# Two drained releases per group instead of seven attached ones, and a second buffer for the histogram operands

## The reference, cut to what matters

```python
h = batch_norm(x @ w1.T + b1, g1, bt1)
src, dst = (edge_index[0], edge_index[1])      # dst is sorted
diff = h[src] - h[dst]
m = jax.ops.segment_max(diff, dst, num_segments=N)
```

## Time and profile before

| | us |
|---|---|
| median of 3 runs | 3649.25 (3648.39 to 3667.12) |
| span of the profiled execution, first to last instruction | 3634.8 |

### The profile page before, as it was taken

The page is one execution under the profiler, slowest core; times in us unless marked ns, Lnnn a source line. Parts: engine busy times, 40 slices in busy tenths (PEclk is TensorE's granted clock), DMA queues, the critical chain, the costliest instruction groups (busy, mean ns, idle before and its releaser), DMA issues. The chain is left out here.

```text
span 3634.8 us, 41575 instructions
## 1 busy us (share of the span) xinstructions
PE 2966.5 (82%) x15504; PEld 2461.7 (68%) x15504; DVE 2207.0 (61%) x4089; ACT 1962.2 (54%) x2741; POOL 1496.1 (41%) x1530
## 2 busy tenths in 40 slices
PE   6578777787877778788887777728988999999998
PEld 5456565665665656566665666527878999999998
DVE  6576666666666666666666666540885556555544
ACT  5356555555555655555555555415165565566554
POOL 1566565565666655556665555561410000000000
PEclk9789898898898998889898898868999999999999
DMA  7355555555555555455555555450213324333331
GB/s 227 114 195 196 181 197 187 194 197 182 194 191 189 189 169 170 167 169 181 170 183 169 171 176 171 160 204 25 61 75 98 118 105 135 128 115 115 115 109 69
DMA packets 164927, 559.97 MB, mean 154 GB/s; under 512 B 31190, under 2 KB 68374, under 8 KB 157556
## 3 DMA queue, kind: packets, MB, share of 16 engines
q1 hardware_dynamic: 87492, 355.23, 26.1%
q0 software_dynamic: 77232, 202.08, 19.5%
HBM read 320.19 MB, written 237.00 MB: 153 GB/s over the span
## 5 line engine op out<-in xcount | busy, mean ns | idle before, releaser
L648 POOL DMA_INDIRECT ring<-runs,src_i x1436 | 1410.4, 982 | 1004.2 <-DVE ring L815 518.7
L999 PE MATMUL ps<-oh,zhl 128*128 128x512 f32 x3136 | 1347.5, 430 | 321.9 <-issue 159.7
L1001 PE MATMUL ps<-oh,zhl 128*128 128x512 f32 x3136 | 1308.0, 417 | 12.8 <-issue 12.5
L670 ACT ACTIVATE oh<-ids,nodeneg 128x512 fp32r<-128x512 f32 x896 | 633.6, 717 | 900.7 <-PE ps L1001 487.4
L999 PEld LDWEIGHTS ps<-oh,zhl 128*128 128x128 f32 x3136 | 642.1, 205 | 515.2 <-issue 186.4
L815 DVE SCALAR_TENSOR_TENSOR ring<-ring,pen 128x256 f32<-128x256 f32 x1564 | 750.4, 480 | 63.5 <-DMA ring<-runs,src_i 32.3
L821 DVE TENSOR_SCALAR oh<-ps,nodef 128x512 fp32r<-128x512 f32 x672 | 501.7, 747 | 403.6 <-PE ps L1001 248.5
L1001 PEld LDWEIGHTS ps<-oh,zhl 128*128 128x128 f32 x3136 | 643.2, 205 | 146.1 <-issue 15.3
L675 ACT ACTIVATE oh<-oh,ones 128x512 fp32r<-128x512 f32 x896 | 613.6, 709 | 0.0
L827 DVE TENSOR_TENSOR oh_lo<-lo,ps 128x896 bf16<-128x896 bf16 x224 | 242.8, 1084 | 328.7 <-remote 302.3
L1569 ACT ACTIVATE av<-ps,vecs 128x896 f32<-128x896 f32 x224 | 246.3, 1100 | 330.4 <-PE ps L191 330.4
(11 more groups left out here) (294 smaller groups left out, 3872.2 us busy)
## 6 DMA issues: line engine op xcount, KB each, us to landing
runs<-ring SPq DMA_DIRECT2D x136, 896.0 KB
fw<-wsp SPq DMA_DIRECT2D x56, 1536.0 KB, 6.5
runs<-ring SPq DMA_DIRECT2D x102, 768.0 KB
ring<-runs,src_i POOLq DMA_INDIRECT x1436
ids<-srcT_d SPq DMA_DIRECT2D x32, 256.0 KB
res_d<-x_all SPq DMA_DIRECT2D x7, 896.0 KB
y<-res_d SPq DMA_DIRECT2D x7, 896.0 KB, 7.0
part<-in_Wx SPq DMA_DIRECT2D x16, 384.0 KB
```

The source lines that it names most:

```text
L648: pool.indirect_dma_start(ring[:, k, :], None, runs[0:N, :], bass.IndirectOffsetOnAxis(ap=src_i[:, STEPS * i + k:STEPS * i + k + 1], axis= ...
L670: act.activation(oh[:, v, :], ids[:, bass.ds(h, 1), :].rearrange("p a n -> p (a n)"), ACT.Abs, bias=nodeneg[:, bass.ds(SLOTS * g + v, 1)]) ...
L999: pe.matmul(ps[:, two + k, :], z_hi(g)[:, v, cols], oh[:, v, :], start=g == 0 and v == 0, stop=False, skip_group_check=True)
L1001: r = pe.matmul(ps[:, two + k, :], z_lo(g)[:, v, cols], oh[:, v, :], start=False, stop=False, skip_group_check=True)
```

## The change

Three edits. (1) The seven attached increments of `s_ohf` per group are gone. Behind slot 3 and behind slot 6 PE executes a drain, which holds it until its work is finished, and then increments `s_ohf` by an instruction of its own. A group now has two releases (`NPART`): slots 0 to 3 wait for the first, slots 4 to 6 for the second (`PART`, `freed`). (2) `oh_lo` and `oh_hi` have two buffers, used in turn. (3) `s_cnt` is no longer incremented; `low_hots` waits for a release of `s_ohf` that implies that the buffer's last reader is done, namely the first release of the group before.

```diff
+PART = (0, 0, 0, 0, 1, 1, 1)
+NPART = 2
...
-        oh_lo = plan.at("oh_lo", [P, NG, P], BF16, p2["oh_lo"])
-        oh_hi = plan.at("oh_hi", [P, NG, NT], BF16, p2["oh_hi"])
+        spot = places["zT"] + STEPS * C * 4
+        oh_lo = [plan.at(f"oh_lo{j}", [P, NG, P], BF16, at) for j, at in enumerate((p2["oh_lo"], spot))]
+        oh_hi = [plan.at(f"oh_hi{j}", [P, NG, NT], BF16, at) for j, at in enumerate((p2["oh_hi"], spot + NG * P * 2))]
...
+        def freed(i, g, v):
+
+            return NPART * (NG * i + g) + PART[v] + 1
...
                 def distance(i, h, g, v):
-                    wait(act, s_ohf, NT * i + SLOTS * g + v + 1)
+                    wait(act, s_ohf, freed(i, g, v))
...
                 def one_hot(i, h, g, v):
-                    wait(dve, s_ohf, NT * i + SLOTS * g + v + 1)
+                    wait(dve, s_ohf, freed(i, g, v))
...
                 def low_hots(i, g):
-                    wait(dve, s_cnt, NG * i + g + 1)
+                    t = NG * i + g + 1
+                    if t >= 2:
+                        wait(dve, s_ohf, NPART * (t - 1) + 1)
                     at = HCOL * i + g * NG
-                    dve.tensor_tensor(oh_lo[:], lo16[:, bass.ds(at, NG)].unsqueeze(2).to_broadcast([P, NG, P]),
+                    dve.tensor_tensor(oh_lo[t % 2][:], lo16[:, bass.ds(at, NG)].unsqueeze(2).to_broadcast([P, NG, P]),
...
                     wait(pe, s_oh, t + 1)
                     for n in range(NG):
-                        r = pe.matmul(ps[:, 0, 0:NT], oh_lo[:, n, :], oh_hi[:, n, :], start=False, stop=False, skip_group_check=True)
-                    r.then_inc(s_cnt, 1)
+                        pe.matmul(ps[:, 0, 0:NT], oh_lo[t % 2][:, n, :], oh_hi[t % 2][:, n, :], start=False, stop=False, skip_group_check=True)
...
-                            r.then_inc(s_ohf, 1)
+                            if v == SLOTS - 1 or PART[v + 1] != PART[v]:
+                                pe.drain()
+                                pe.sem_inc(s_ohf, 1)
...
-                pe.sem_inc(s_ohf, SLOTS)
+                pe.sem_inc(s_ohf, NPART)
```

More of the change, by code:

```diff
@@ L274, in build @@
         hi16 = plan.at("hi16", [P, HR * HCOL], BF16, p2["hi16"])
-        oh_lo = plan.at("oh_lo", [P, NG, P], BF16, p2["oh_lo"])
-        oh_hi = plan.at("oh_hi", [P, NG, NT], BF16, p2["oh_hi"])
+        spot = places["zT"] + STEPS * C * 4
+        oh_lo = [plan.at(f"oh_lo{j}", [P, NG, P], BF16, at) for j, at in enumerate((p2["oh_lo"], spot))]
+        oh_hi = [plan.at(f"oh_hi{j}", [P, NG, NT], BF16, at) for j, at in enumerate((p2["oh_hi"], spot + NG * P * 2))]
+        assert spot + NG * P * 2 + NG * NT * 2 <= places["zT"] + MAT
         iota = plan.at("iota_i", [P, P], I32, places["part_hi"])
@@ L831, in high_hots @@
                     at = HCOL * i + g * NG
-                    dve.tensor_tensor(oh_hi[:], hi16[:, bass.ds(at, NG)].unsqueeze(2).to_broadcast([P, NG, NT]),
+                    dve.tensor_tensor(oh_hi[(NG * i + g + 1) % 2][:], hi16[:, bass.ds(at, NG)].unsqueeze(2).to_broadcast([P, NG, NT]),
                                       io_hi.unsqueeze(1).to_broadcast([P, NG, NT]), ALU.is_equal).then_inc(s_oh, 1)
@@ L892, in _ @@
                                 src_i[:, STEPS:STEPS * (PG + 1)].rearrange("p (g s) -> p g s", s=STEPS)[:, :, PSLOT:STEPS]).then_inc(s_srcf, 1)
-                dve.memset(oh_lo[:], 0.0)
-                dve.memset(oh_hi[:], 0.0).then_inc(s_oh, 1)
+                dve.memset(oh_lo[0][:], 0.0)
+                dve.memset(oh_hi[0][:], 0.0).then_inc(s_oh, 1)
                 dve.tensor_copy(nodef[:], node_i[:])
```

## The result

The changed kernel took 3836.76 us (median; 3823.76 to 3838.47) where the kernel before, run beside it on the same chip, took 3648.82 (3645.08 to 3667.12). The ratio is 1.051, with a 95% interval of 1.0479 to 1.054: slower by 188 us, outside the range, on the side that had 13%. The profiled execution's span is 3834.9 us, 2.0 us under the time of that run (3836.92); before it was 3634.8. So of the 14.4 us that the prediction puts on top of the span about 2 lie around it, and the rest is difference from run to run.

What follows compares the result with a forecast made beforehand. Edge loop bound by a closed ring of waits, with PE's releases often late, not by one engine's work. Rounds from 68.4 to 56.0 us save 397 us over 32: span 3237.8 plus 14.4 gives 3252 us, range 3150 to 3470.

Steps and rivals of the forecast that it cites:

- the side that had 13%: The outcome that the changed kernel is slower than the kernel before, given a chance of 0.13.
- the 14.4 us: Whole kernel: the median stands 14.4 us above the profiled span, added to 3237.8 to give 3252 us.
- what goes is their lateness: PE in the edge loop: removing seven attached increments saves no issue time but ends releases coming 3.42 and 8.0 us late.
- The third rival: Edge loop: the increment behind the drain is late too; with 3.42 us delay the time is 3758 us; chance 0.08.
- the ring: Edge loop: second release, ACT's matrices, then PE's slots and drains to the next release, 6.7 us a group against PE's 7.6.
- The fourth rival: Edge loop: release is prompt already, long waits come from elsewhere and stalls stay, giving 3862 us; chance 0.07.
- The drains' own cost: PE behind slots 3 and 6: 0.42 and 0.53 us, so 0.95 a group, 6.65 a round, 213 us for the loop.
- Coarser release: Edge loop: slots released up to 2.7 us later cost nothing by itself, given 0.9 us slack; 1.6 a round put down.
- The operand buffers: DVE before low_hots: 329 us of idling goes, cost nothing; the gain is no sum of its own but in the ring.
- one rival: Edge loop: POOL's limit of 52.1 us is reached, the round comes to 53 us and the time to 3156; chance 0.12.
- The 56.0 forecast for the round: Edge loop: PE's 47.7 us of gapless work plus 6.65 for drains plus 1.6 for coarser release, against 68.4 before.
- The signs listed for a wrong prediction: Edge loop: gaps behind drains over 0.8 us, or ACT still starting microseconds after PE's increment.

Runs made afterwards that it cites:

- e5: The changed kernel as it is, run again beside the kernel before in a set with late completions: 3764.52 us, ratio 1.0484.
- e7: The changed kernel without gathers (POOL only counts its semaphores up), in a set with late completions: 3028.13 us, one run.
- e1: The changed kernel without drains, its two releases per group attached to matmuls, in a prompt set: 3084.45 us, ratio 1.0017 to the kernel before.
- e6: The changed kernel without drains, its two releases per group attached to matmuls, in a late set: 3659.93 us, ratio 1.0176 to the kernel before.
- e10: The kernel before with only the two operand buffers added, seven attached increments per group kept, in a prompt set: 3076.79 us, ratio 0.9997.
- e12: The changed kernel as it is, run beside the kernel before in a prompt set: 3084.94 us, ratio 1.002.
- e16: The kernel before with nine buffers for the 0/1 matrices instead of seven, in a late set: 3610.47 us, ratio 0.9954.
- e15: The changed kernel with plain DMAs of 128 consecutive rows from SP's queue replacing POOL's gathers, in a late set: 3021.72 us, one run.

## Why the prediction was wrong, step by step

**The step that failed** is "what goes is their lateness". Rows 3 to 5 showed rightly that a release came 3.42 and 8.0 us late, and that elsewhere it took 0.04. From that I put the delay into the attachment. It is in PE's completion: the drain above was late by 5.5 us, and 144 of 448 were late. The one drain that I had the earlier trace rows lies behind the loop, where few gathers run, and its 0.06 us was taken for a property of drains. It was one of the place.

**The price of a late drain.** The third rival had the mechanism, but took the delay into the ring only, on top of 6.7 us. A drain holds PE as well, so it stands on top of PE's own list: 7 x (6.65 + 0.63) + 1.1 + 16.8 = 68.9 us. The rest to the measured 74.8 is 5.9 us of slow clock and of waits behind the stops (e5 in the same way: 52.1 + 483 / 32 = 67.2 of 72.5); I did not split it further. The rival named 3758; measured was 3837. The fourth rival's 3862 is nearer, for another reason: its premise, prompt release, is false in that profile.

**The drains' own cost** was sized at 0.95 us a group and is 0.63 [e7]: 4.4 and not 6.65 us a round, 141 and not 213 us for the loop. The timeline of e7 splits it. Behind slot 3 the next two matmuls start 0.47 and 0.33 us on instead of twice 0.23: 0.34 us, where the sum had 0.42. Behind slot 6 the histogram starts 0.47 us on, 0.24 too many, where the sum had 0.53. The term that is not there is the 0.23 us for the pace of 14 short instructions: from the histogram's start to the next matmul's 0.19 us pass (1007.81 to 1008.00), as the prediction says of a stream without drains. The last 0.05 of the 0.63 are not split.

**Coarser release** "costs nothing by itself": 0.2% with prompt completions (1.0017, e1), but 1.8% together with the buffers where they are late (e6). With slots 0 to 3 on one release, one late word stops four slots and not one. That reading is argued, the 63.5 us are measured.

**The operand buffers** did what was said: idling 0.0 before L837. The gain was to come through the ring and did not.

**What was late next.** POOL's limit was nearer than PE's, as one rival said, but I had it too low: a round has 46 steps and 42 gathers, not the 45 and 41 that stand above (32 x 42 + 2 x 46 = 1436, the count in the earlier trace rows; the ring has 46 slots, a partition 34 x 46 = 1564 edges). So the limit is 42 x 1.27 = 53.4 and not 52.1 us. Prompt loops show it, each from its first and last histogram: e1 (1870.9 - 127.3) / 32 = 54.5, e10 (1867.0 - 125.9) / 32 = 54.4, the changed kernel 54.8. The 56.0 forecast for the round was thus near to what the program does when nothing is late; the kernel before does the same then, and 0.2% faster. (A slip beside it: PE's gapless work, 7 x 6.65 + 33.0 / 31, is 47.6 and not 47.7.)

**The signs listed for a wrong prediction** came: ACT did not start microseconds after the increment, but the gaps behind drains were over 0.8 us.

**The rule of the skill.** The Trainium skill, PSUM — Partial Sum Buffer, section Engine vs sequencer instructions, has the increment attached and the drain as a barrier only. As advice it holds here, where the prediction had set the row against it: attached against drained is 104.6 us better where completions are late (e6 against e5) and makes no difference where they are prompt (1.0017 for e1 and 1.002 for e12, each against its own set, with overlapping intervals). That nothing would be late by it does not hold.

**What stays open.** What switches a chip between the two behaviours: one chip had 3079.05 in one set and 3629.89 in the next. Whether it is POOL's work for a gather, its queue, or the scattered rows that delays PE's completions, and whether the slow issue seen in e6 and e16 is the same thing. Every run here has a span from the profiler, so none shows whether the lateness exists while nothing is recorded; that the late profiles also lose records makes the recording itself a rival that was not tested. Also open is where the rest of the late time goes: from the kernel before (3634.8 us of span) to e10 (3079.4) the rounds explain 32 x (68.4 - 54.4) = 448 us, and some 107 lie outside them. Whether pauses on POOL cure it, and what seven attached increments with two buffers do in a late set. No kernel here beats both: the nine matrices gain 0.46% in a late set and nothing in a prompt one.

## What to carry to other kernels

A delay between an instruction and its waiter belongs to whatever carries the message until an experiment has changed the carrier; a drain reads the same completion and holds its engine besides. Take the price of a barrier from a place with the same neighbours, here POOL's gathers, not from the quiet end of a block. Where the same kernel can take 3080 or 3630 us, compare only runs taken side by side, and ask of each experiment whether the disturbance was there at all: thirteen of the eighteen kernels ran where it was not.

## What the runs showed of the hardware that was not expected

PE's completions can be told late, by up to 9.35 us, and 11 us in e5, whose longest drain took 13.857 us where the median is 3.185:

```profile
L1013 PEldq DRAIN  x448: 2015/3185/13857, 148.8 to 2460.8; - x150
```

This happened only beside POOL's indirect gathers: 144 and 143 of 448 with them, none without them (e7, one run) and none with more bytes a second from SP's queue (e15, one run), in sets where the kernel before was slow. The increments of ACT were not late with them, but 193 to 270 of the 896 records of `distance` are missing. It is not always there: whole sets with the same gathers had none. And a drain on POOL behind gathers cost 2.58 us of idling, so that gathers can't be paced cheaply in that way.
